# Sorting half of the items inside the attention before a top-1 expert stage, one copy for the latent and gate columns, and last two stages without a drain

## The reference

```python
def mla_attention(x, ...):                       # 16 heads of 8, causal
    q = x @ Wq.T
    latent = layernorm(x @ Wdkv.T, ln_g, ln_b)   # 64 columns
    k, v = latent @ Wuk.T, latent @ Wuv.T
    ...
def moe(x, gate_w, gate_b, W1, b1, W2, b2):      # 4 experts, one per row
    logits = x @ gate_w.T + gate_b
    onehot = one_hot(argmax(logits, axis=-1), 4)
    h = relu(einsum('btd,ehd->bteh', x, W1) + b1)
    y = einsum('bteh,edh->bted', h, W2) + b2
    return einsum('bted,bte->btd', y, onehot)
x = x + mla_attention(rmsnorm(x, norm1_w), ...)
x = x + moe(rmsnorm(x, norm2_w), ...)
```

## Time and profile before

| what | us |
|---|---|
| median of 3 runs | 1251.22 |
| the runs | 1248.94, 1251.22, 1252.82 |
| profiled execution | 1253.27 |
| its span, first to last instruction | 1251.5 |

### The profile page before, as it was taken

One profiled execution on the slowest core, in us unless ns is written; L12 is line 12 of the kernel. 1 busy time (PEld: TensorE's weight loads), 2 busy tenths in 40 slices (PEclk: granted clock), 3 DMA queues, 4 the chain that ended last, 5 costly groups with the idle time before them and its releaser, 6 DMA issues. The chain is left out here.

```text
span 1251.5 us, 36853 instructions
## 1 busy us (share of the span) xinstructions
PE 1054.8 (84%) x13632; PEld 790.6 (63%) x13632; DVE 874.8 (70%) x2781; ACT 615.6 (49%) x1465; POOL 362.2 (29%) x896
## 2 busy tenths in 40 slices
PE   2999998782796599969997989997899999970996
PEld 2888887672554477734445768884357888850896
DVE  4687774998634677769997758885755877753574
ACT  2588874565123266622223435554843445433674
POOL 1122221122013133300001212222434565545743
PEclk9999999896798599989998979997877999995898
DMA  9700000000000500030000000000020000002710
GB/s 287 197 9 3 4 3 1 1 2 1 1 2 1 163 2 3 3 135 1 1 1 1 1 2 3 3 3 2 1 77 2 3 3 3 3 2 74 242 32 24
DMA packets 36318, 40.66 MB, mean 32 GB/s; under 512 B 7325, under 2 KB 30625, under 8 KB 35888
## 3 DMA queue, kind: packets, MB, share of 16 engines
q1 hardware_dynamic: 32384, 31.77, 8.6%
q0 software_dynamic: 2752, 6.38, 1.5%
q10 hardware_dynamic: 1008, 0.16, 0.1%
HBM read 26.85 MB, written 11.84 MB: 31 GB/s over the span
## 5 line engine op out<-in xcount | busy, mean ns | idle before, releaser
L690 PE MATMUL ps<-qTm,kT 32*128 32x512 f32 (+1 forms) x1024 | 252.5, 557 | 2.0 <-ACT probs L593 1.6
L722 PE MATMUL ps<-kT,qTm 32*128 32x128 f32 x3200 | 253.2, 293 | 0.8 <-DVE kT L422 0.8
L722 PEld LDWEIGHTS ps<-kT,qTm 32*128 32x128 f32 x3200 | 229.0, 204 | 6.1 <-issue 3.4
L513 POOL CAST nm<-neg_max 128x16 bf16<-128x16 f32 (+1 forms) x132 | 27.0, 205 | 416.5 <-DVE neg_max L381 157.0
L593 ACT ACTIVATE probs<-ps 128x1024 f32<-128x1024 f32 x72 | 73.8, 1025 | 121.6 <-PE ps L732 121.6
L394 DVE TENSOR_REDUCE neg_max<-ps 128x8 f32<-128x1024 f32 x72 | 87.9, 1220 | 62.4 <-PE ps L722 62.4
L879 PE MATMUL ps<-probs,v_wide 128*32 128x128 f32 x3200 | 117.4, 281 | 4.9 <-DVE o_sb L443 1.7
L690 PEld LDWEIGHTS ps<-qTm,kT 32*128 32x128 f32 x1024 | 85.9, 191 | 48.8 <-issue 40.1
L389 DVE TENSOR_REDUCE neg_max<-ps 128x4 f32<-128x512 f32 x128 | 82.1, 683 | 36.2 <-PE ps L722 36.1
L589 ACT ACTIVATE probs<-ps,bias_col 128x512 f32<-128x512 f32 x128 | 81.0, 684 | 37.3 <-PE ps L732 37.3
L408 DVE TENSOR_TENSOR qTm<-ps,hmask 128x512 f32<-128x512 f32 (+1 forms) x132 | 73.2, 555 | 35.8 <-ACT nmT L571 20.4
(11 more groups left out here) (410 smaller groups left out, 2523.1 us busy)
## 6 DMA issues: line engine op xcount, KB each, us to landing
sorted_rows<-late SPq DMA_DIRECT2D x2, 2479.5 KB, 15.6
late<-in_ctx SPq DMA_DIRECT2D x4, 1024.0 KB, 10.9
late<-in_ctxT SPq DMA_DIRECT2D x2, 2048.0 KB
x_all<-in_x SPq DMA_DIRECT2D x4, 512.0 KB, 7.1
kv_all<-sorted_rows SPq DMA_DIRECT2D x2, 783.0 KB, 6.1
q_all<-sorted_rows SPq DMA_DIRECT2D x1, 1044.0 KB, 9.0
kv_all<-sorted_rows SPq DMA_DIRECT2D x2, 522.0 KB, 4.2
late<-in_W1T SPq DMA_DIRECT2D x1, 1024.0 KB, 5.3
```

The lines of the kernel that those rows point to most:

```text
L690: nc.tensor.matmul(ps[:, bank, at:at + N], kT[rows_of(g), k, :], qTm[rows_of(g), k, 0:N], start=True, stop=False, skip_group_check=True)
L722: last = nc.tensor.matmul(dst, qTm[rows_of(g), k, 128 * i:128 * i + 128], kT[rows_of(g), k, :], start=False, stop=True, skip_group_check=True)
```

## The change

The moments and the choice are made for each batch of 16 items by itself. For batch 0 they are split into generator parts that DVE runs at the ends of steps 24, 26, 27, 28 and 29 of the attention (`CHOOSE_AT` gives the number of parts); PE counts in step 28, ACT makes the inverse root in step 25 (Ln, then Exp of -0.5 times it, then a Newton step on DVE) and scales two items in each step from 27 on; POOL sorts one item a step from step 30 and three a step from 34; SP waits for the 16 DMAs and loads batch 0's tiles before its phase_end. Only batch 1 is left for the expert stage. POOL's end of the attention is a wait for its 32 joins in place of a drain. The last phase has no `phase_end`, and SP waits for the stores in POOL's place. In the latent stage ACT copies 68 columns at once, and POOL multiplies all gate columns by the rows' scale afterwards. The choice's arithmetic past this is the same and left out.

```diff
+CHOOSE_AT, ROOT_AT, COUNT_AT, SORT_AT = {24: 5, 26: 8, 27: 8, 28: 7, 29: 8}, 25, 28, 30
...
         def attention_vector(dve, L, count, heads, normalise, post):
...
                 if L not in LOW:
                     done(dve, "nmT_ready", b + 3, count)
+                if L == "L4" and b + 6 == COUNT_AT:
+                    for _ in read_counts(dve, 0, ps[:, 7, 400:468]):
+                        pass
...
+                if L == "L4" and time_of(items) in CHOOSE_AT:
+                    part = opening if time_of(items) < COUNT_AT else closing
+                    for _ in itertools.islice(part, CHOOSE_AT[time_of(items)]):
+                        pass
+            if L == "L4":
+                opening, closing = choose_first(dve, 0), choose_last(dve, 0)
...
         def attention_gpsimd(pool, L, count, heads, raw):
...
                 nc.gpsimd.tensor_tensor(rows[:, b, JOIN:ROW_NO], x_all[:, b, :], z_all[:, b, :],
-                                        ALU.add)
+                                        ALU.add).then_inc(sem("mo_summed"), 1)
...
+                sorting = iter(range(*BATCHES[0]))
+
+                def step(items):
+                    for lag, stage in work:
+                        if lag in items:
+                            stage(*items[lag])
+                    if time_of(items) >= SORT_AT:
+                        for b in itertools.islice(sorting, 1 if time_of(items) < SORT_AT + 4 else 3):
+                            sort_row(pool, b)
...
         def attention_scalar(act, L, count, heads, raw, post):
...
+                if L == "L4":
+                    if time_of(items) == ROOT_AT:
+                        root_inverse(act, 0)
+                    if time_of(items) > ROOT_AT + 1:
+                        for b in itertools.islice(scaling, 2):
+                            scale_row(act, b)
...
         def attention_tensor(pe, L, count, heads, mask_parts, mask, post_w):
...
                     last = turn_max(None) if L not in LOW else product() if post else None
+                    if L == "L4" and at_one + 1 == COUNT_AT:
+                        count_places(pe, 0, ps[:, 7, 400:468])
...
-        def phase_end(engine):
+        def phase_end(engine, sorting=False):
...
-            engine.drain().then_inc(sem("phase_done"), 1)
+            if sorting:
+                engine.wait_ge(sem("mo_summed"), B)
+                engine.sem_inc(sem("phase_done"), 1)
+            else:
+                engine.drain().then_inc(sem("phase_done"), 1)
...
         def latent_gpsimd(pool):
...
             steps(pool, B, [(4, query)])
+            pool.wait_ge(sem("la_raw"), B)
+            nc.gpsimd.tensor_tensor(rows[:, :, GATE:JOIN], lat_raw[:, :, LATENT:LATENT + N_EXP3],
+                                    inv_ln[:].unsqueeze(2).broadcast_to([128, B, N_EXP3]), ALU.mult)
...
             def take_latent(b, k):
                 act.wait_ge(sem("la_halves"), b + 1)
-                nc.scalar.activation(rows[:, b, GATE:JOIN], ps[:, 2 + k, 320:320 + N_EXP3], ACT.Copy,
-                                     scale=inv_ln[:, b:b + 1])
-                nc.scalar.activation(lat_raw[:, b, :], ps[:, 2 + k, 256:320], ACT.Copy).then_inc(sem("la_raw"), 1)
+                nc.scalar.activation(lat_raw[:, b, :], ps[:, 2 + k, 256:320 + N_EXP3], ACT.Copy
+                                     ).then_inc(sem("la_raw"), 1)
...
+        def choose_first(dve, i):
...
+            yield q(V.memset(v["whole"], 128.0 * n))
+            q.count(V.tensor_tensor(even, st[:, :, 1], st[:, :, 1], ALU.mult))
+            q.count(V.tensor_tensor(odd, st[:, :, 4], st[:, :, 4], ALU.mult))
+            yield q(V.tensor_tensor(var, st[:, :, 2], st[:, :, 5], ALU.add))
+            q.count(V.tensor_scalar(var, var, 1.0 / D, 1e-6, ALU.mult, ALU.add))
+            yield q(V.tensor_tensor(even, even, odd, ALU.add))
+            yield q(V.scalar_tensor_tensor(var, even, 0.5, var, ALU.mult, ALU.add))
+            c = moments_taken["v"] = moments_taken.get("v", 0) + 1
+            yield dve.sem_inc(sem("variance"), 1)
+            dve.wait_ge(sem("deviation"), c)
+            yield q(V.scalar_tensor_tensor(odd, guess, -0.5, guess, ALU.mult, ALU.mult))
+            yield q(V.tensor_tensor(odd, odd, var, ALU.mult))
+            yield q(V.scalar_tensor_tensor(inv, odd, 1.5, guess, ALU.add, ALU.mult))
+            dve.sem_inc(sem("mo_scale_set"), 1)
...
+        def root_inverse(act, i):
+
+            c = moments_taken["s"] = moments_taken.get("s", 0) + 1
+            v = chain_of(i)
+            act.wait_ge(sem("variance"), c)
+            nc.scalar.activation(v["low"], v["var"], ACT.Ln).then_inc(sem("mo_logged"), 1)
+            act.wait_ge(sem("mo_logged"), i + 1)
+            nc.scalar.activation(v["guess"], v["low"], ACT.Exp, scale=-0.5).then_inc(sem("deviation"), 1)
+
+        def scale_row(act, b):
+
+            i = 0 if b < BATCHES[1][0] else 1
+            if b == BATCHES[i][0]:
+                act.wait_ge(sem("mo_scale_set"), i + 1)
+            act.wait_ge(sem("mo_summed"), b + 1)
+            nc.scalar.activation(z_all[:, b, :], z_all[:, b, :], ACT.Copy, scale=inv_all[:, b:b + 1]
+                                 ).then_inc(sem("mo_normed"), 1)
...
+        def sort_row(pool, b):
+            i = 0 if b < BATCHES[1][0] else 1
+            first, n = BATCHES[i]
+            if b == first:
+                pool.wait_ge(sem("mo_placed"), i + 1)
+            pool.wait_ge(sem("mo_normed"), b + 1)
+            nc.gpsimd.indirect_dma_start(
...
         def expert_gpsimd(pool):
...
-            pool.wait_ge(sem("mo_stored"), 16 * TILES3)
...
-        def expert_tiles(sp):
+        def expert_tiles(sp, batch=1):
             for i, at, n, (tile_loaded, before) in tile_loads():
+                if i != batch:
+                    continue
...
+            if batch == 1:
+                sp.wait_ge(sem("mo_stored"), 16 * TILES3)
...
+        def free_rows(sp):
+            sp.wait_ge(*after("first_turned", B))
+            sp.wait_ge(*after("v_ready", B))
...
-                 sync=expert_loads),
+                 sync=lambda e: (expert_loads(e), free_rows(e), expert_tiles(e, 0))),
...
-                         (8, "ln", None), (9, "ln", None), (10, "ln", None), (12, "ln_rms6", "ln"),
-                         (14, "rms", None)):
+                         (8, "ln", None), (9, "ln", None), (10, "ln", None), (12, "ln_rms6", "ln")):
...
-                phase_end(engine)
+                if phase is phases[-1]:
+                    return
+                phase_end(engine, name == "gpsimd" and phase is phases[-2])
```

More of the change, by code:

```diff
@@ L51, in whole_steps, with time_of @@
         step({lag: (t - lag, (t - lag) % RING) for lag in range(last + 1) if 0 <= t - lag < count})
+def time_of(items):
+    lag, (item, _) = next(iter(items.items()))
+    return item + lag
 def wait_reuse(engine, signal, item, depth, per_item=1):
@@ L1851, in batch_of, with chain_of @@
             return 0 if g < FIRST_TILE[1] else 1
-        def choose(dve, i):
+        def chain_of(i):
+            first, n = BATCHES[i]
+            m, f, fb = N_EXP3 * n, chain_f[:, i, :], chain_b[:, i, :]
+            v = {"lg": f[:, 0:m].rearrange("p (b e) -> p b e", e=N_EXP3),
+                 "eq": f[:, 64:64 + m].rearrange("p (b e) -> p b e", e=N_EXP3),
+                 "top": f[:, 128:128 + n], "chosen": f[:, 144:144 + m], "run": f[:, 208:208 + m],
+                 "place": f[:, 272:272 + m], "counts": f[:, 272:340], "before": f[:, 336:340], "after": f[:, 337:341],
+                 "whole": f[:, 340:341], "tiles": f[:, 348:352], "start": f[:, 352:356], "off": f[:, 356:360],
+                 "place_f": f[:, 360:360 + n], "expert_f": f[:, 392:424], "earlier": fb[:, 0:m],
+                 "chosen_b": fb[:, 64:64 + m]}
+            for j, name in enumerate(("even", "odd", "var", "low", "guess")):
+                v[name] = f[:, 456 + 16 * j:456 + 16 * j + n] if j < 3 else f[:, 16 * (j - 3):16 * (j - 3) + n]
+            return v
@@ L1862, in choose @@
[L1862 to L1869, removed]
@@ new lines, in choose_first @@
+            dve.wait_ge(sem("deviation"), c)
[3 more added lines that the diff above has]
+            dve.sem_inc(sem("mo_scale_set"), 1)
+            lg, eq, top, chosen = v["lg"], v["eq"], v["top"], v["chosen"]
+            yield q(V.tensor_tensor(lg, rows[:, items, GATE:JOIN], inv.unsqueeze(2).broadcast_to(full), ALU.mult))
@@ new lines, in choose_last @@
+        def choose_last(dve, i):
+            n = BATCHES[i][1]
+            q = Seq(dve, sem("vector_step"), moments_taken)
+            V, v = nc.vector, chain_of(i)
+            before, tiles, start, off, place, expert_f = (v[name] for name in (
+                "before", "tiles", "start", "off", "place", "expert_f"))
+            yield q(V.tensor_tensor(tiles, v["after"], before, ALU.subtract))
+            yield q(V.tensor_scalar(tiles, tiles, 1.0 / 128, 127.0 / 256, ALU.mult, ALU.add))
```

(11 more changed lines are left out.)

112 lines of the change are left out of this document (60 added, 52 removed).

## The result

The changed kernel takes 1233.4 us (median of 4 runs, 1231.95 to 1234.43) against 1251.01 for the one before: a ratio of 0.9856, 95% interval 0.9836 to 0.9876, or 17.6 us less. On another chip the same two gave 0.9849 (0.9835 to 0.9862). The profiled execution took 1233.19 us, with a span of 1231.4.

A forecast was written before the change was run, and what follows sets the result against it. The prediction saw PE full in attention and tile loop, with a 37.4 us chain between them. Its terms, -3.7 + 5.1 + 8.5 - 27.0 - 1.1 = -18.2 off the median of 1251.22, gave 1233.0 us, range 1224 to 1243.

The forecast's parts named there:

- A: Latent stage: one copy of the gate and latent columns shortens the loop's items; -3.7 us (-5 to 0).
- B: Inside the attention: half the choice adds DVE length, table loads and slowing beside POOL's cuts; +5.1 us (1.5 to 9.6).
- D: Barrier to first expert tile: the 37.4 us chain becomes 10.4; -27.0 us (-28.3 to -25).
- C: Attention's end: sorts delay the last cut, then landing and loads delay the barrier; +8.5 us (+6 to +12).
- rival 4: Attention's end: placing or scaling is late, so all 16 sorts stand behind the attention; 1250 us, chance 0.05.
- The row with 1.05: Profile row behind the cuts' +1.0: a DVE operation beside a one-input POOL operation took 1.05 us, a fifth more.
- rival 2: In the attention, POOL's cuts stop DVE wholly, each of five pieces waiting one out: +9.6 us there, 1237.5; chance 0.2.
- E: Kernel's end: POOL's last drain begins earlier, as SP waits for the stores; -1.1 us (0 to -6.9).
- rival 1: Kernel's end: the last drain goes with the phase's end, -6.9 us there, 1227.2 in all; chance 0.22.
- Rival 3: Attention: PE's pauses in steps 25 to 29 drop its clock to 1.2 GHz for the rest; +28 us, 1261; chance 0.05.

The follow-up runs named there:

- e1: Kernel before with only the latent stage's part (one copy of 68 columns, POOL's one multiply): 1247.4 us against 1251.5, ratio 0.9968.
- e7: Changed kernel with all 16 sorts of batch 0 behind POOL's last join of the attention: 1250.41 us, ratio 1.0004 to the kernel before.
- e4: Changed kernel with SP loading batch 0's tiles in the expert stage, behind the attention's barrier: 1230.37 us, ratio 0.9823 to the kernel before.
- e5: Changed kernel with the latent stage as before (two copies per item, no multiply on POOL): 1239.12 us, ratio 0.9901 to the kernel before.
- e11: Changed kernel without POOL's cuts in steps 24 to 29 and with Copy in place of Ln: 1226.52 us, ratio 0.9811 to the kernel before.
- e2: Changed kernel without POOL's twelve cuts (causal mask) in attention steps 24 to 29: 1231.74 us, ratio 0.9848 to the kernel before.
- e8: Changed kernel with the last stage's phase_end and POOL's wait for the stores kept as in the kernel before: 1235.67 us.
- e3: Changed kernel with Copy in place of Ln in both batches, so no table change: 1231.23 us, ratio 0.9832 to the kernel before.

## Why the prediction was right, point by point

The time came out at 1233.4 where 1233.0 was given, and the medians differ by 17.6 where the sum was -18.2. In the profiled pair the six terms make -15.1, and -17.4 with A at the 4.0 us that e1 measures. The parts of some terms were further off than their sums, and that the time came out within 0.4 us is luck: B alone was 1.5 off, and can be 1.3 more from one profile to the next.

**D and C, the large terms, were right** to 0.3 us: -26.7 for -27.0, and 3.8 + 4.6 = +8.4 for +8.5. Both were built from single rows of before, and these held: 1.28 us a sort, 2.5 to 2.7 to land, five loads in 2.5, ACT's scalings at 0.30. Within D two steps were wrong and cancelled: Ln's load did not run ahead of the barrier but behind Ln's own wait (1133.52, +1.3), and the register load and the row copy, put down for 1.0, lay beside the scalings. Within C the last cut started at 1118.36 where 1118.7 was given. PE's sum behind it ends 2.7 us late, near the 2.5 of the forecast, but the arithmetic lost 3.8: the rest is the clock of 1.2 GHz from 1119.5 on, which no term held (a pair of PE's products behind the sum takes 0.78 in place of 0.46). In e7, with its cut on time, the same stretch loses 1.8 at that clock. What follows took 4.6 and not 6.0, so C's total was met in part by luck. e7 gives rival 4's price (1250 worked out, 1250.4 measured; from the last join to the barrier, 25.6 and 25.2) and so shows that the gain lies in sorting beside the attention. e4 shows that 3.2 of C's 8.4 bought nothing: the tile was not needed so early.

**A was the right size.** -3.7 was given; e1 measures -4.0 (-2.0 to -6.1), and the stage is 3.5 us shorter than in e5. The loop's items take 0.66 us in place of 0.82, as forecast. The profiled pair has -1.7, since the clock in that stage rises at other moments from run to run (54.8 to 57.1 us for the same code).

**B was +5.1 and came out at +6.6, with its parts mis-sized.** The +2.4 for DVE's length measured 2.5, with one operation still blocked (e11). The +1.7 for two table loads measured 1.0 with the cuts out (e2 against e11): the loads are there, two of 1.28, and PE waits 1.3 us for the exps behind them. "A cut has one input, so I take the nearer: +1.0" is the step that failed: the cuts cost 2.9 (e2), the clock's fall included. The row with 1.05 was the wrong neighbour: a cut stops DVE to its end, once in each piece. Why that row's operation was not stopped stays open. By its rows it ran from 375.76 to 376.81, wholly inside POOL's operation (375.53 to 377.45), so that this pair barely overlapped, as rival 2 has it, is not what they show.

The Trainium skill, "SBUF — State Buffer", "Who interferes with whom", says that a DVE instruction with two SBUF inputs contends with a GpSimd instruction that reads SBUF, and the trace of the cuts agrees: 0.95 in place of 0.17 us, ended with the cut. On the other page of the Trainium skill, "ScalarE: Activation LUTs", "Table sets: the hidden batching unit", the trace differs: Ln then Exp took two loads, at 1133.52 and 1135.04, not one, so the two loads that B counted were the right choice.

**E.** -1.6 for -1.1; rival 1 is out, as the drain only moved (e8). The drain ends 5.8 us after POOL's last store has left it, 1.1 sooner than in the kernel before, as forecast; the other 0.5 is what stood between the drain and the end of the span there (0.7, now 0.2), which the forecast left out.

**The rivals in the attention.** Rival 2's mechanism was real, at 3.9 us of blocked time rather than 5.5. Rival 3, which had been given 28 us, was right in part: PE's clock did fall to 1.2 GHz behind its waits, but for 3.4 us and not for the rest of the stage, in each of the nine profiles of the changed attention with its cuts on (6.8 in e7), and in neither of the two without them. Which of the waits brings it on is not shown: in e2 the 1.3 us for ACT is there and the clock stays up, in e3 it is gone and the clock falls.

**What neither side of the sum held:** -1.9 ahead of the latent stage and -3.2 at the attention's start. Neither is the change's doing. The first stretch takes 857.4 to 863.7 us in the thirteen profiles, whose code is the same up to there. The second belongs to the profile of before, which took 1253.27 where its median is 1251; taking the difference off the median, and not off that execution, kept it out of the forecast.

## What to carry to other kernels

Work moved into a stage's idle time can be paid twice, at the engine that takes it and through what runs beside it there: here 2.5 us for DVE's length and 2.9 for POOL's cuts, which stopped it, the clock's fall included. Price it by the operation that runs beside it, not by its length alone. A serial chain between two stages is best shortened by finding what its first consumer needs: here 16 sorts, beside the attention, gave the whole gain of 17 us (e7), while loads ahead of the barrier gave nothing and cost 3. When an edit puts a wait in front of a barrier, ask who needs its result and when; what isn't needed for another 7 us belongs behind it.

## What was not expected of the hardware

A cut on POOL, with one input, held DVE's two-input operations and even a cast of 128x16 (0.82 us in place of 0.17) until it ended, while another one-input operation of POOL's didn't. Waits of PE of 0.7 to 1.8 us were followed by 3.4 us at 1.2 GHz in a stage where PE is otherwise always busy. Ln followed by Exp loaded two tables. POOL's drain at the end took 5.8 us after all stores had landed (e8), and it ended 5.8 us after the last store left POOL in the changed kernel, where nothing waited for the landing: leaving out the wait and the stage's last synchronisation gave 1.6 us, and no more.
